# An mLSTM and ternary feed-forward block: masks, the split of x(1) and a value unit re-placed in the opening of the kernel

## The chip, the cores and the metric

One core of one Trainium2 chip runs one program. The metric is the device time of one execution in microseconds (us), as the median of several executions. Engines: TensorE (PE, with PEld for its weight loads), VectorE (DVE), ScalarE (ACT), GpSimd (POOL), and SyncE (SP), which here only issues DMAs.

## What is computed

For 16 sequences of 512 tokens with 512 features, in float32:

```
x = x + mlstm_layer(layernorm(x))        # 8 heads, q and k 256 wide, v 512 wide
x = x + ffn(layernorm(x))                # 512 -> 2048 -> 512, exact gelu, ternary weights

mlstm: i = cap(x Wig + big), f = cap(x Wfg + bfg), cap(z) = 15 tanh(z / 15)
       C_t = F C_{t-1} + I k v^T,  n_t = F n_{t-1} + I k,  h = (q C) / max(|q n|, exp(-m))
       y = (sigmoid(x Wog) * gamma * (h - mean) / sqrt(var + eps)) Wout      # mean, var per head
ternary: w -> sign(w) where |w| >= 0.7 mean|w|, else 0
```

## The kernel before

Each engine has a program written out by hand; they meet by semaphores alone, and each queue is strictly in order. A sequence is handled as 4 tiles (T = 4) of 128 tokens, the mLSTM in chunks of 128 tokens: within a chunk a head's scores (a 128x128 block for each chunk) are weighted with decays and masked to earlier tokens. float32 products are made of float16 halves (HI and LO) in three passes. The mLSTM part of sequence b runs beside the feed-forward part of sequence b - 1. Sequence 0 has no such partner: its mLSTM part runs beside the preparation of the weights, and this opening is what the change rewrites. `first` and `not run_f` mark it, and `isinstance(b, int) and b == 0`.

Preparation: w1 and w2 come as 16 pairs of row blocks. For pair q the division by the threshold (`small_gone`, VectorE, L1261, for w1; `small2_gone`, ScalarE, L826, for w2) is followed by `ternary_transpose(q)` on TensorE (into one of two banks of `pf`) and `ternary_out(q)` on ScalarE (L835), which writes the signs and frees the bank. The output weights go through `weights_out` (TensorE), `weights_hi` (ScalarE, L783) and `weights_lo` (VectorE, L1235).

The order around the change, for sequence 0:

- **Decays.** ScalarE exponentiates two heads at a time (`decay`, L1010). VectorE multiplies each head's scores from PSUM by its decays (`weigh`, L1475). GpSimd then masks two heads at a time (`earlier_only`, L653, an affine select over 128x1024), waiting until both have been weighed. `chunk_heads(0)` on TensorE waits for the last mask.
- **x(1).** VectorE normalises sequence 1 (`norm_apply`, L1297) and splits it (`split_x1`, L1307) into halves in `g32` and `qT`, ahead of the first `weigh`; SP moves them, transposed, to `xT` (`transpose_x1`, L544).
- **Head statistics.** `head_stats(0, j)` on VectorE (L1485), for chunks j = 0 to 3: sums of the columns (`hsum`), the norm (`den`) with a floor added as a tensor-scalar operation (L1526, and L1551 in `stats_in_bank` for j of 2 and 3), the centred heads (`cent`, L1528, L1547), `gated(j - 1)` (L1573) and the variance. Beside it for each j: ScalarE squares the centred heads (`squares`, L1051), GpSimd raises the variance to a power and multiplies (`head_norm`, L684 and L687), VectorE gates the product (L1579), ScalarE makes its high half (`gated_hi`, L1070), GpSimd its low half (`gated_lo`, L691), and SP transposes it to `hoT`, from which TensorE computes `project(0, j)`. `head_stats(0, j)` for j of 2 and 3 first waits for `gated_lo(j - 2)`.
- **TensorE** (`first_heads`, L2212): scores, transposes of w1 and w2 between the chunks, six filler products ahead of pair 5 and eighteen ahead of pair 10 (`busy_until`, L2194: products of an identity whose result is not used), the four projections, and before the third of these the gates and two value units of sequence 1 (`gates(1)`, `late_values(1, 1)`, `tokens(1, U_V, ...)`). The bank of `project(0, 3)` is freed by ScalarE's `value(1, 0)` (L953, L963), which is queued behind the exponential of sequence 1's gates (L873); that one needs `gate_minus(1)` on VectorE (L1342), which waits until the last transposed tile `hoT[3]` is there.

`busy_until` in the code:

```
def busy_until(q, times):
    pe.wait_ge(pf_free[q % 2], q // 2)
    keep_busy(pf[:, q % 2, :], times)
    ternary_transpose(q)
```

## Time and profile before

| what | value |
|---|---|
| median of 3 runs | 1740.2 us (1740.05 to 1741.62) |
| the profiled execution: its own time | 1742.3 us |
| its span | 1740.6 us |
| mean granted TensorE clock | 0.996 |
| TensorE busy | 1707.5 us, 98% of the span |
| VectorE, ScalarE, GpSimd busy | 1437.6, 1059.6, 606.6 us |
| end of the opening (start of `project(0, 3)`) | 116.01 us |

Times in the rows are microseconds from the span's start. "Granted clock" is TensorE's clock as the throttle let it through, 1 being 2.4 GHz and 0.5 being 1.2 GHz. A row of the timeline groups neighbouring instructions of one line; the bracket at its end is the time for which the engine was idle before it and what ended that.

### The profile page before, as it was taken

What the parts mean: (1) busy time and instruction counts of PE and PEld (TensorE: products, weight loads), DVE (VectorE), ACT (ScalarE), POOL (GpSimd) and SP (SyncE); (2) the same over time, 40 slices, a digit from 0 to 9 for tenths busy, and PEclk for the clock granted to TensorE, in tenths of its full rate; (3) what the DMA queues carried; (4) which work ended last, traced back from release to release, by engine and by line L of the source; (5) the groups of instructions that cost most, each with busy time, mean ns of one, the idle gap of its engine ahead of it and who ended that gap; (6) DMA issues with size and microseconds to landing.
All of it is one profiled execution on the core that took longest, in us unless ns stands there. A gap on an engine that the chain in (4) does not pass through costs nothing.

```text
span 1740.6 us, 31380 instructions
## 1 busy us (share of the span) xinstructions
PE 1707.5 (98%) x12028; PEld 841.4 (48%) x12028; DVE 1437.6 (83%) x2528; ACT 1059.6 (61%) x1769; POOL 606.6 (35%) x477
## 2 busy tenths in 40 slices
PE   6899999999999999999999999999999999999999
PEld 4554445444444444445444444444444444454455
DVE  7888788897888978789887888988789788886872
ACT  6978375473746638375573746648375573847643
POOL 1242514335241442514235241442514235241430
PEclk9999999999999999999999999999999999999999
DMA  8736253442725326253442725336262442625120
GB/s 321 219 89 167 58 141 72 117 120 56 170 60 127 87 80 160 58 154 59 120 117 56 171 60 126 87 92 152 55 161 61 110 119 56 148 59 132 33 55 25
DMA packets 294981, 187.45 MB, mean 108 GB/s; under 512 B 239136, under 2 KB 260640, under 8 KB 289712
## 3 DMA queue, kind: packets, MB, share of 16 engines
q1 hardware_dynamic: 293248, 182.30, 41.7%
q10 hardware_dynamic: 1584, 3.15, 0.5%
q8 instruction: 95, 1.56, 0.4%
q14 instruction: 54, 0.44, 0.1%
HBM read 96.47 MB, written 20.23 MB: 67 GB/s over the span
## 4 chain that ended last, share of the span: by engine, by line
PE 81%; DVE 8%; DMA 3%; SPq 3%; issue 2%; POOL 1%; ACT 1%; POOLq 0%; DVEq 0%; ACTq 0%
PE pf L2073 24%; PE pf L2057 22%; PE pa L1926 17%; PE pa L1902 7%; PE psh L1926 5%; SPq L530 2%; PE psh L2013 2%; DMA kT<-shared 1%; PE psh L1968 1%; PE psh L2047 1%; DVE gT L1633 1%; PE pa L2013 1%; DVE dec L1482 1%; PE pa L1893 1%; PE psh L2009 1%
## 5 line engine op out<-in xcount | busy, mean ns | idle before, releaser
L2073 PE MATMUL pf<-w2T,gT 128*128 128x512 f16 x2048 | 505.8, 379 | 0.0
L2057 PE MATMUL pf<-x2T,w1T 128*128 128x512 f16 x1920 | 422.0, 379 | 0.0
L2057 PEld LDWEIGHTS pf<-x2T,w1T 128*128 128x128 f16 x1920 | 185.4, 98 | 222.5
L2073 PEld LDWEIGHTS pf<-w2T,gT 128*128 128x128 f16 x2048 | 195.5, 97 | 177.0
L1633 DVE SCALAR_TENSOR_TENSOR gT<-g,wscale,gT 128x512 f16<-128x512 f32 x240 | 208.5, 871 | 22.5 <-ACT gT L1046 20.2
L1926 PE MATMUL pa<-wT,xT 128*128 128x512 f16 x960 | 212.8, 379 | 0.6 <-ACT sig L970 0.6
L1043 ACT ACTIVATE g<-pf,b1c 128x512 f32<-128x512 f32 x240 | 164.1, 684 | 72.5 <-PE pf L2057 56.6
L1046 ACT ACTIVATE gT<-g,wscale 128x512 f16<-128x512 f32 x240 | 173.3, 722 | 7.9
L1926 PE MATMUL pa<-wT,shared 128*128 128x512 f16 x768 | 176.2, 379 | 1.6 <-DMA shared<-qT 0.8
L1051 ACT ACTIVATE ktok<-kT 128x512 f32<-128x512 f32 x64 | 40.4, 631 | 216.4 <-DVE kT L1528 214.9
L1902 PE MATMUL pa<-xT,wT 128*128 128x512 f16 x768 | 171.4, 379 | 0.0
L1010 ACT ACTIVATE dec<-dec,gtok 128x128 f32<-128x128 f32 x512 | 154.4, 392 | 0.0
L1926 PEld LDWEIGHTS pa<-wT,xT 128*128 128x128 f16 x960 | 93.9, 98 | 113.6 <-ACT sig L970 1.1
L679 POOL TENSOR_TENSOR dec<-dec 128x1024 f16<-128x1024 f32 x30 | 71.9, 2398 | 200.4 <-ACT dec L1061 200.4
L1926 PE MATMUL psh<-wT,xT 128*128 128x512 f16 x576 | 129.7, 379 | 0.0
L702 POOL TENSOR_TENSOR x1b<-xres,b2r 128x512 f32<-128x512 f32 x64 | 80.6, 1269 | 125.2 <-DVE xres L1590 113.8
L684 POOL TENSOR_TENSOR hinv<-hvar,half 128x8 f32<-128x8 f32 x64 | 104.8, 1638 | 49.0 <-DVE hvar L1570 49.0
L691 POOL TENSOR_TENSOR qT<-kT,qT 128x512 f16<-128x512 f32 x64 | 74.1, 1157 | 132.5 <-ACT qT L1070 132.5
L1926 PEld LDWEIGHTS pa<-wT,shared 128*128 128x128 f16 x768 | 74.8, 98 | 92.4 <-DMA shared<-qT 1.8
L661 POOL TENSOR_SCALAR_AFFINE_SELECT dec<-dec 128x1024 f32<-128x1024 f32 x64 | 92.2, 1441 | 70.0 <-DVE dec L1482 69.8
L1902 PEld LDWEIGHTS pa<-xT,wT 128*128 128x128 f16 x768 | 74.5, 98 | 86.3
L651 POOL TENSOR_TENSOR rstd<-ve,half 128x4 f32<-128x4 f32 x16 | 16.6, 1037 | 279.6 <-DVE ve L1292 279.6
(246 smaller groups left out, 2705.2 us busy)
## 6 DMA issues: line engine op xcount, KB each, us to landing
dec<-gate_r SPq DMA_DIRECT2D x32, 1024.0 KB, 6.1
xin<-L_attn_x SPq DMA_DIRECT2D x16, 1024.0 KB, 6.0
out<-x1b SPq DMA_DIRECT2D x64, 256.0 KB, 2.3
xres<-L_attn_x SPq DMA_DIRECT2D x16, 512.0 KB, 4.3
xres<-L_attn_x SPq DMA_DIRECT2D x32, 256.0 KB, 3.0
qw<-gate_w SPq DMA_DIRECT2D x128, 48.0 KB, 2.0
s<-state_w SPq DMA_DIRECT2D x60, 97.5 KB, 2.4
qw<-kT SPq DMA_DIRECT2D x120, 48.0 KB, 2.0
```

The costliest lines, as they stand in the source:

```text
L661: nc.gpsimd.affine_select(out=rows_of, in_=rows_of, compare_op=ALU.is_ge, fill=0.0, base=0, pattern=[[0, 2 * T], [1, P]], channel_multipli ...
L684: nc.gpsimd.tensor_tensor(hinv[:, :], hvar[:, :], half[:, :], ALU.pow).then_inc(pool_a, 1)
L691: nc.gpsimd.tensor_tensor(head_parts[j % 2][:, LO, :], cent[j % 2], head_parts[j % 2][:, HI, :], ALU.subtract).then_inc(ho_lo[j], 1)
L702: nc.gpsimd.tensor_tensor(x1b[:, t, :], xres[:, t, :], b2r[:, :], ALU.add).then_inc(x1b_ok, 1)
L1010: last = nc.scalar.activation(dec[:, h, tok(j)], dec[:, h, tok(j)], ACT.Exp, bias=gtok[:, j, ROW_C, h:h + 1])
L1043: nc.scalar.activation(g32[:, f % 2, :], pf[:, use % 2, :], ACT.Gelu, bias=b1c[:, f:f + 1], scale=1.0 / X_SCALE).then_inc(pf_free[use % 2], 1)
L1046: nc.scalar.activation(gT[:, HI, f, :], g32[:, f % 2, :], ACT.Copy, scale=wscale[:, W_GELU:W_GELU + 1]).then_inc(g_hi, 1)
L1633: nc.vector.scalar_tensor_tensor(gT[:, LO, f, :], g32[:, f % 2, :], wscale[:, W_GELU:W_GELU + 1], gT[:, HI, f, :], ALU.mult, ALU.subtract) ...
L1902: last = nc.tensor.matmul(bank, wT[:, ws, k, col:col + P], xT[:, xs, :, k, :], start=(k == 0 and n == 0), stop=(k == KD - 1 and n == 2))
L1926: last = nc.tensor.matmul(bank, src[:, xs, k, :], wT[:, ws, k, col:col + D], start=(k == 0 and n == 0), stop=(k == KD - 1 and n == 2))
L2057: last = nc.tensor.matmul(bank, w1T[:, k, tok(f)], x2T[:, part, :, k, :], start=(k == 0 and part == HI), stop=(k == KD - 1 and part == LO))
L2073: last = nc.tensor.matmul(bank, gT[:, part, f, tok(t)], w2T[:, f, :], start=(f == 0 and part == HI), stop=(f == NF - 1 and part == LO), sk ...
```

## The change

In the opening alone, apart from one operation of the head statistics that changes its form in all sequences:

1. GpSimd masks the decays of sequence 0 as soon as ScalarE has made them, not the weighted scores; `weigh` waits for the mask, and `chunk_heads(0)` for the weighing.
2. The halves of x(1) lie in `xres`. The high half is made right after `norm_apply(1)`, the low half behind the fourth `weigh`. The loads of the residual into `xres` wait until x(1) has been transposed.
3. Head statistics: for j of 0 and 1 the centring takes the sum with a factor in one operation and stands ahead of the norm's steps; the floor is added as a tensor-tensor operation with the scalar broadcast; `weights_lo` of the first two output weights moves into `head_stats(0, 1)`, ahead of its centring.
4. TensorE: the second group of scores stands before the transposes of pairs 2 and 3. The unit `late_values(1, 1)` moves from ahead of `tokens(1, U_V, ...)` into the place of the eighteen fillers and writes to `pf`; ScalarE copies it there.
5. ScalarE: `decay(0, 6)` before `ternary_out(0)`; `squares(0)` before `small2_gone(9)`; `ternary_out(9)` up, `small2_gone(12)` and `(13)` down; the wait of `gated_hi(0, 0)` for x(1) goes.

```diff
-x1_halves = [... for part in (g32, qT)]
+x1_halves = [... for part in (xres[:, 0:T // 2, :], xres[:, T // 2:T, :])]
...
 def residual(b, tiles):                       # SP, sequence 0
                     sp.wait_ge(pa_fill, pa_filled(b, score_use(NH - 1)))
+                    sp.wait_ge(x1T_loaded, 32)
...
 def earlier_only(b, n):                       # GpSimd
-                for h in (2 * n, 2 * n + 1):
-                    if in_ps(h):
-                        pool.wait_ge(ps_free[h % 2], ps_done(b, h))
-                    else:
-                        pool.wait_ge(pa_free[h % 2], pa_done(b, score_use(h)))
+                if isinstance(b, int) and b == 0:
+                    pool.wait_ge(d_ok, 2 * n + 2)
+                else:
+                    for h in (2 * n, 2 * n + 1):
...
 def gates(b, fb):                             # ScalarE
-                value(b, 1)
+                if not (isinstance(b, int) and b == 1):
+                    value(b, 1)
...
 def opening():                                # ScalarE
                 decay(0, 4)
+                decay(0, 6)
                 ternary_out(0)
-                decay(0, 6)
...
 def gated_hi(b, j):                           # ScalarE
-                if isinstance(b, int) and b == 0 and j == 0:
-                    act.wait_ge(x1T_loaded, 32)
...
 def sequence(b, fb, ahead):                   # ScalarE
                     ternary_out(5)
+                    squares(b, 0)
                     small2_gone(9)
                     ternary_out(6)
                     small2_gone(10)
-                    squares(b, 0)
                     ternary_out(7)
                     weights_hi(*USES_OUT[0:2])
                     small2_gone(11)
...
                 if not run_f:
                     ternary_out(8)
-                    small2_gone(12)
+                    ternary_out(9)
                 squares(b, 2)
...
                 gated_hi(b, 1)
                 if not run_f:
-                    ternary_out(9)
-                    small2_gone(13)
+                    value(1, 1)
                     ternary_out(10)
+                    small2_gone(12)
                 squares(b, 3)
                 if not run_f:
                     ternary_out(11)
+                    small2_gone(13)
                 gated_hi(b, 2)
...
-            def split_x1():                   # VectorE
+            def split_x1_hi():
                 dve.wait_ge(xn_ok, 2 * T)
+                dve.wait_ge(s_abs, ABS_RES)
                 nc.vector.tensor_scalar(x1_halves[HI], xin[:, :, :], X_SCALE, None, ALU.mult).then_inc(x1_hi, 1)
+            def split_x1_lo():
                 dve.wait_ge(x1_hi, 1)
-                dve.wait_ge(qw_ok, 1)
...
 def weigh(b, n):                              # VectorE
-                dve.wait_ge(d_ok, at(b, NH, n + 1))
+                if isinstance(b, int) and b == 0:
+                    dve.wait_ge(masked, n // 2 + 1)
...
 def head_stats(b, j, ch, waiting=None, between=None):      # VectorE, sequence 0, j of 0 and 1
                     nc.vector.tensor_reduce(*columns)
                     nc.vector.scalar_tensor_tensor(den_of, *own_norm).then_inc(dve_a, 1)
+                    if between is not None:
+                        between()
+                    dve.wait_ge(dve_a, ch.next())
+                    nc.vector.scalar_tensor_tensor(by_head(cent[j % 2]), per_head(hsum[:, :], DHV), -1.0 / DHV, heads,
+                                                   ALU.mult, ALU.add).then_inc(cent_ok, 1)
+                    nc.vector.scalar_tensor_tensor(den_of, norms, -1.0, den_of, ALU.mult, ALU.max).then_inc(dve_a, 1)
+                    dve.wait_ge(dve_a, ch.next())
+                    norm_floor(ch)
+                    head_variance(b, j, ch, waiting)
+                    return
...
-                nc.vector.tensor_scalar(den[:, :], den[:, :], head_scale[:, 1:2], None, ALU.add).then_inc(dve_a, 1)
+                nc.vector.tensor_tensor(den[:, :], den[:, :], head_scale[:, 1:2].to_broadcast([P, NH]), ALU.add).then_inc(dve_a, 1)
...
 def sequence(b, fb, ahead):                   # VectorE
                     norm_apply(b + 1, range(T))
+                    split_x1_hi()
                     chunk_decay(b)
                     thresholds()
                     small_gone(0, 1)
                     key_tokens(b)
                     small_gone(2, 3)
-                    split_x1()
...
                     if not run_f and n == H4:
+                        split_x1_lo()
                         small_gone(4)
                     weigh(b, n)
...
                     head_stats(b, 0, ca, lambda: small_gone(7))
-                    head_stats(b, 1, ca)
-                    weights_lo(*USES_OUT[0:2])
+                    head_stats(b, 1, ca, None, lambda: weights_lo(*USES_OUT[0:2]))
                     head_stats(b, 2, ca)
...
 def chunk_state(b, j):                        # TensorE, j of 0
-                    pe.wait_ge(masked, at(b, NH // 2, NH // 2))
+                    if isinstance(b, int) and b == 0:
+                        for n in (H4, H4 + 1):
+                            pe.wait_ge(ps_free[n % 2], ps_done(b, n))
...
 def first_heads():                            # TensorE
                 scores(0, 0)
+                scores(0, 1)
                 ternary_transpose(2)
                 ternary_transpose(3)
-                scores(0, 1)
                 ternary_transpose(4)
...
                 weights_out(2, 3)
-                busy_until(10, 18)
+                x_ready(1)
+                pe.wait_ge(ps_free[1], at(1, PS_USES[1], 0))
+                pe.wait_ge(pf_free[1], 5)
+                token_products(pf[:, 1, :], xT[:, :, 1, :, :], C_V).then_inc(ps_fill, 1)
+                ternary_transpose(10)
+                pe.wait_ge(ps_free[1], at(1, PS_USES[1], 1))
                 ternary_transpose(11)
                 weights_ready(*USES_OUT)
                 project(0, 0)
                 ternary_transpose(12)
                 project(0, 1)
                 ternary_transpose(13)
-                x_ready(1)
                 gates(1)
                 ternary_transpose(14)
                 ternary_transpose(15)
-                late_values(1, 1)
                 tokens(1, U_V, xT[:, :, 0, :, :], C_V)
                 project(0, 2)
                 project(0, 3)
```

## Rows read from the trace of the kernel before

**Rows 1.** Stretches: length, busy us of PE, PEld, DVE, ACT, POOL, granted clock, DMA.
```profile
68.00:80.00 12.00, 7.12 (x86) 4.76 (x86) 10.83 (x18) 11.69 (x19) 5.06 (x4) 0.72 1.04 235
...
99.20:116.00 16.80, 15.90 (x104) 7.80 (x105) 11.24 (x23) 13.57 (x18) 9.45 (x8) 1.00 0.32 64
116.00:1736.00 1620.00, 1616.02 (x11291) 785.11 (x11292) 1345.48 (x2332) 966.62 (x1624) 574.88 (x438) 1.00 0.41 99
```

**Rows 2.** Timeline of TensorE: start, us, engine and line, operation, count, idle before.
```profile
76.73 2.77 PE L1850 MATMUL pf<-wT,ident 128*128 128x512 f16 x6
...
80.24 1.97 PE L2005 MATMUL pa<-vaug,dec 128*128 128x65 f32 x16 [0.17 <-POOL dec L661]
...
93.73 4.05 PE L1850 MATMUL pf<-wT,ident 128*128 128x512 f16 x18
...
116.01 2.75 PE L1926 MATMUL pa<-wT,shared 128*128 128x512 f16 x12 [0.60 <-ACT vaug L963]
```

**Rows 3.** Timeline of VectorE up to the last weighing.
```profile
59.74 0.17 DVE L1427 COPY fcol<-qw 128x6 f32<-128x6 f32 x1 [1.67 <-DMA qw<-gate_w]
...
62.52 1.42 DVE L1267 TENSOR_SCALAR x2T<-gT,w 128x1024 f16<-128x1024 f32 x2
...
67.11 1.22 DVE L1310 TENSOR_SCALAR g<-xin 128x2048 f16<-128x2048 f32 x1
68.37 2.29 DVE L1313 SCALAR_TENSOR_TENSOR qT<-xin,g 128x2048 f16<-128x2048 f32 x1
70.58 0.68 DVE L1482 SCALAR_TENSOR_TENSOR dec<-psh,dec 128x512 f32<-128x512 f32 x1
...
73.08 1.28 DVE L1482 SCALAR_TENSOR_TENSOR dec<-pa,dec 128x512 f32<-128x512 f32 x2
...
77.20 1.28 DVE L1482 SCALAR_TENSOR_TENSOR dec<-pa,dec 128x512 f32<-128x512 f32 x2
```

**Rows 4.** The masks of sequence 0, all instructions of line 661 up to 120 us.
```profile
L661 POOL TENSOR_SCALAR_AFFINE_SELECT dec<-dec x4: 1093/1292/1482, 73.3 to 78.6; 128x1024 f32<-128x1024 f32 x4
```

**Rows 5.** VectorE: the divisions by line, then its timeline in chunks 1 and 3.
```profile
L1267 DVE TENSOR_SCALAR x2T<-gT,w x8: 742/748/1578, 62.5 to 85.1; 128x1024 f16<-128x1024 f32 x8
...
88.51 0.96 DVE L1526 TENSOR_SCALAR den<-den,head_scale 128x8 f32<-128x8 f32 x1
...
90.37 0.69 DVE L1579 SCALAR_TENSOR_TENSOR kT<-kT,sig 128x512 f32<-128x512 f32 x1
...
91.78 1.41 DVE L1248 SCALAR_TENSOR_TENSOR wT<-pa,gcol,wT 128x512 f16<-128x512 f32 x2
...
107.06 0.69 DVE L1579 SCALAR_TENSOR_TENSOR kT<-kT,sig 128x512 f32<-128x512 f32 x1 [0.50 <-POOL kT L687]
```

**Rows 6.** Timeline of VectorE and GpSimd in sequence 1, side by side in time.
```profile
188.72 2.10 DVE L1530 SCALAR_TENSOR_TENSOR den<-den,head_scale 128x8 f32<-128x8 f32 x1
...
188.13 2.66 POOL L679 TENSOR_TENSOR dec<-dec 128x1024 f16<-128x1024 f32 x1 [0.42 <-ACT dec L1061]
```

**Rows 7.** Timeline of ScalarE.
```profile
60.39 2.44 ACT L1010 ACTIVATE dec<-dec,gtok 128x128 f32<-128x128 f32 x8
...
79.05 1.14 ACT L833 ACTIVATE x2T<-gT,w 128x1024 f16<-128x1024 f32 x1
80.11 1.02 ACT L844 ACTIVATE w1T<-pf 128x1024 f16<-128x1024 f16 x1
...
87.49 1.26 ACT L795 ACTIVATE wT<-pa,gcol 128x512 f16<-128x512 f32 x2
...
102.36 0.63 ACT L1070 ACTIVATE qT<-kT 128x512 f16<-128x512 f32 x1 [0.32 <-DVE kT L1579]
```

**Rows 8.** GpSimd by groups, 56 to 120 us: count, busy us, mean ns, idle before.
```profile
L684 POOL TENSOR_TENSOR hinv<-hvar,half 128x8 f32<-128x8 f32 x4 | 6.6, 1638 | 6.6 <-DVE hvar L1570 6.6
...
L691 POOL TENSOR_TENSOR qT<-kT,qT 128x512 f16<-128x512 f32 x4 | 4.6, 1159 | 7.4 <-ACT qT L1070 7.4
L687 POOL TENSOR_TENSOR kT<-kT,hinv 128x512 f32<-128x512 f32 x4 | 4.2, 1042 | 0.3
```

More of the change, by code:

```diff
@@ L195, in block_program @@
         square = head_sum[:, :, 0:DHV]
-        x1_halves = [part[:, :, :].bitcast(F16).rearrange("p g s -> p (g s)").rearrange("p (t d) -> p t d", d=D) for part in (g32, qT)]
+        x1_halves = [part[:, :, :].bitcast(F16).rearrange("p g s -> p (g s)").rearrange("p (t d) -> p t d", d=D) for part in (xres[:, 0:T // 2, :], xres[:, T // 2:T, :])]
         q16 = (kT[:, :, :].bitcast(F16).rearrange("p g s -> p (g s)")[:, 0:2 * HG * LATE]
@@ L403, in block_program @@
         wbank = [ps[:, 0, :], pf[:, 0, :], pf[:, 1, :], ps[:, 1, :], pa[:, 0, :], pa[:, 1, :]]
+        ABS_RES = 3
         USES_V, USE_GATE, USES_QK, USES_O, USES_OUT = range(4), 4, range(5, 9), range(9, 13), range(13, 17)
@@ L958, in value @@
                     act.wait_ge(ps_fill, at(b, PS_FILLS, F_V + 1))
-                    bank, free = ps[:, 1, :], ps_free[1]
+                    bank, free = pf[:, 1, :] if isinstance(b, int) and b == 1 else ps[:, 1, :], ps_free[1]
                 else:
@@ L1480, in weigh, with head_stats @@
                     dve.wait_ge(pa_fill, pa_filled(b, score_use(n)))
-                dve.wait_ge(d_ok, at(b, NH, n + 1))
+                if isinstance(b, int) and b == 0:
+                    dve.wait_ge(masked, n // 2 + 1)
+                else:
+                    dve.wait_ge(d_ok, at(b, NH, n + 1))
                 nc.vector.scalar_tensor_tensor(dec[:, n, :], score_bank(n), SCORE_SPLIT, dec[:, n, :],
                                                ALU.mult, ALU.mult).then_inc((ps_free if in_ps(n) else pa_free)[n % 2], 1)
-            def head_stats(b, j, ch, waiting=None):
+            def head_stats(b, j, ch, waiting=None, between=None):
                 if not (isinstance(b, int) and b == 0 and j == 0):
@@ L1532, in head_stats, with norm_floor @@
                 head_variance(b, j, ch, waiting)
+            def norm_floor(ch):
+                nc.vector.tensor_tensor(den[:, :], den[:, :], head_scale[:, 1:2].to_broadcast([P, NH]), ALU.add).then_inc(dve_a, 1)
+                dve.wait_ge(dve_a, ch.next())
+                nc.vector.scalar_tensor_tensor(den[:, :], den[:, :], head_scale[:, 2:3], den[:, :], ALU.mult, ALU.mult).then_inc(dve_a, 1)
+                dve.wait_ge(dve_a, ch.next())
             def in_bank(b, j):
@@ L1977, in chunk_state @@
                         take_pa(b, U_H0 + g)
-                    pe.wait_ge(masked, at(b, NH // 2, NH // 2))
-                    if not (isinstance(b, int) and b == 0):
+                    if isinstance(b, int) and b == 0:
+                        for n in (H4, H4 + 1):
+                            pe.wait_ge(ps_free[n % 2], ps_done(b, n))
+                    else:
+                        pe.wait_ge(masked, at(b, NH // 2, NH // 2))
                         pe.wait_ge(vlo_ok, at(b - 1, T, T))
```

6 lines of the change are left out of this document (5 added, 1 removed).

## Prediction

> **What bounds the kernel now.** The table of stretches comes first [rows 1]. From 116 us to the end TensorE is busy 1616.02 of 1620 us at full clock, so nothing behind 116 us can be shortened by this change: it can only move the moment at which that block begins. Before it TensorE is not the bound: 7.12 of 12 us are busy from 68 to 80 us, at a granted clock of 0.72.
>
> TensorE's own rows tell what holds it there [rows 2]. The heads of the first chunk begin at 80.24, released by the last mask on the decays. Eighteen fillers run from 93.73 for 4.05 us and compute nothing. `project(0, 3)` begins at 116.01 after 0.60 us of waiting for ScalarE's copy of the values of sequence 1 out of a bank. That copy stands behind the exponential of sequence 1's gates, which needs the last transposed head tile, which comes from `gated(0, 3)` on VectorE at 107.06 [rows 5]. Between 107.06 and 116.01 lie 8.95 us of dependent steps that the change leaves alone (ScalarE's and GpSimd's halves, a transposing DMA, gate steps, exponential, copy). So what decides is when `gated(0, 3)` runs; the four chunks before it are a chain through VectorE, ScalarE and GpSimd. The two moved pieces of TensorE work count only if that chain keeps up.
>
> **Up to the first heads.** Removed ahead of the first weighing: both halves of the split of x(1), 67.11 to 70.58 on VectorE, 3.4 us [rows 3]. The high half (1.22 us) goes into 1.67 us in which VectorE waits for a DMA before 59.74: free. If that cover were gone it would cost its 1.22. The low half (2.29) goes behind the fourth weighing. Its old place has no cover, its new one lies beside the scores of heads 4 to 7, for which VectorE would wait about 1 us anyway.
>
> The masks now need only the decays. ScalarE makes the first pair by 62.83 [rows 7], the second, after a copy of 0.5 and as many exponentials, by about 65.8, where VectorE runs the threshold divisions and, between them, the two key operations [rows 3]. Masks and divisions block one another: a division takes 742 ns undisturbed and 1578 at worst, the worst one standing beside a mask [rows 5], and a mask 1093 to 1482 [rows 4]. The price of a mask that gets in ahead of such an instruction is therefore 0.84 us (1578 less 742); the other bound is 0 (VectorE first, GpSimd waits, which hurts nobody: a mask has some microseconds to spare). Two masks fall there. I take both at 0.85, so 1.7 us, since both orders of arrival put the mask between two queued VectorE instructions. First weighing: 70.58 - 3.4 + 1.7 = 68.9. Fourth ends 3.8 later (as now, 70.58 to 74.36) at 72.7; low half to 75.0; division 4 to 75.7; weighings 4 to 7 take 2.5, to 78.2, against 78.4 now [rows 3].
>
> TensorE meanwhile: scores of heads 4 to 7 begin with the end of the fourth weighing, and now scores and the transposes of one pair of w1 fill the time from there to the fillers, 74.36 to 76.73, 2.3 us with their releases [rows 2, 3]. Pairs 2 and 3, transposed ahead of the scores before, now stand behind them, so pair 2 is done at 72.7 + 2.3 = 75.0, and ScalarE can write the signs of pairs 2 and 3 only then, at 1.0 us apiece [rows 7]: 76.0 and 77.0. The six fillers wait for the second of these. From the first filler to the first head it is 3.5 us now, of which 0.17 is the wait for the mask, with the clock at its lower level (six fillers in 2.77 against eighteen in 4.05) [rows 2]: 77.0 + 3.3 = 80.3. The first heads begin at 80.2 or 80.3, as now: **the wait for the masks is gone, and the signs ahead of the fillers take its place.** Bounds: 79.1 if no mask gets in the way and the clock is up, 81 if the lower clock lasts into the heads.
>
> **Chunk 0.** Centring comes two steps sooner (0.65 us), which only makes ScalarE's squares ready sooner; VectorE's own queue is one 0.2 us instruction shorter. Gain 0.2.
>
> **Chunk 1, the costly place.** `weights_lo` of the first two output weights (1.41 us) [rows 5] moves from behind chunk 1 into its middle, ahead of the centring. It waits for ScalarE's `weights_hi`, at 87.49 now [rows 7]. ScalarE's list up to there has changed too: the squares of chunk 0 stand before `small2_gone(9)`, and ScalarE, a strict queue, sits idle for them from about 82.8 to 84.0. From there: squares 0.6 (as long as a high half, 0.63), then `small2_gone` 1.04, signs 0.92 and both once more (spacings of instructions of 1.14 and 1.02) [rows 7], so `weights_hi` begins at about 88.5 and the first is done at 89.2. VectorE reaches the wait at 87.5 and idles 1.7; the two `weights_lo` end at 90.7, the centring runs from 90.6 (now 89.50, right behind the 0.96 us instruction) and `gated(0, 0)` at 91.9 against 90.37 now [rows 5]. Behind the waiting VectorE instruction stand the centring, the squares and variance of chunk 1 and `gated(0, 0)`. The shorter list gives 0.9 of it back (0.96 to 0.17, and one of 0.16). The net is **+1.5**.
>
> **Chunks 2 and 3.** One turn of the loop is: `gated` 0.69, ScalarE's high half 0.63, GpSimd's low half 1.16, power 1.64, product 1.04 [rows 5, 7, 8], with some 0.2 of releases: 5.4 us. Today the turns take 5.63 (90.37 to 107.06 in three). So once the loop binds a turn can shrink by 0.2 and no more: -0.4 for two. The other way, ScalarE's list now has `ternary_out(11)` and `small2_gone(13)` together before `gated_hi(2)`, and also the copy of the moved unit: `gated_hi(2)` starts about 0.9 late (bounds 0 and 1.6). The new wait on TensorE, for ScalarE's copy of the moved unit, has `ternary_transpose(11)` and `project(0, 0)` behind it; the copy is queued behind `gated_hi(0, 1)`, so it is there near 99.3, while `project(0, 0)` waits for `weights_lo` on VectorE until about 100.3 in any case: nothing.
>
> **Queues passed.** On SP the transposition of the low half now waits for 75.0 instead of 70.5, and the load of x(2), the third and fourth loads of w2 rows and the residual wait behind it, the residual also for its landing, about 80. The first reader of x(1) is the moved unit near 95, of the w2 rows a ScalarE instruction near 100, of the residual the first output near 104. On GpSimd the masks pass nothing. I cost all this at 0; without that cover each would cost the 4.5 us of its lateness at most.
>
> The other saving announced, the floor of the norm as a tensor-tensor operation, is worth little. The 0.96 us instruction at 88.51 stands beside GpSimd's product (0.23 is its normal length) [rows 5], but VectorE instructions with two SBUF operands are stretched by GpSimd just as well: the 128x8 one at 188.72 takes 2.10 and ends with GpSimd's 188.13 + 2.66 [rows 6]. The new form has two SBUF operands, so in chunks 2 and 3 I count nothing for it. The Trainium skill (SBUF — State Buffer, "SBUF: two separate sides") says the same in general: the pair of ports shared with GpSimd is an exclusive lock, also for a VectorE operation with two SBUF inputs against a GpSimd one that reads SBUF. By the row alone, which shows tensor-scalar operations stretched and says nothing of the new form, chunks 2 and 3 would gain up to 0.5 each until the loop binds, about 0.6 together, and the sum would be +1.7 where I take +2.3.
>
> **Sum.** 0 (start) - 0.2 + 1.5 - 0.4 + 0.9 = +1.8; the same schedule laid out instruction by instruction with these durations, which also carries the small idle gaps, gives +2.6. I take +2.3. TensorE: 3.9 us of fillers go, the unit of 2.6 us leaves the stretch before `project(0, 2)`; both turn into waiting, for signs 9 before the unit and for the gates' bank and the values' copy before 116. All behind `project(0, 3)` moves with it, in one piece.
>
> The profiled execution took 1742.3 us around its span of 1740.6, 2.1 above the median of the runs, 1740.2. It would become 1744.6; the median 1742.5. About 0.2%, 3.5 us, is what a measurement of this kernel tells from no change.
>
> **Rivals.**
> *No contention.* Masks slip into gaps, `weights_hi` is early enough for VectorE to idle 0.5 instead of 1.7: the start wins 1.1, chunk 1 loses 0.3. Sum about 0 to -0.5, plus 0.9 on ScalarE: 1740.5. For it: masks now mostly delay themselves. Against: the 1.09 us masks have no gap in VectorE's row from 62.5 to 66.
>
> *The chain shortens as meant.* Start -1.1, chunk 0 -0.2, chunk 1 -0.9 (`weights_lo` finds its input ready), two turns -0.2 each, ScalarE in time: -2.6, 1737.6. TensorE would allow it: it has 2.6 + 0.6 to give. Against: ScalarE is busy 11.69 of 12 us up to 80 us [rows 1], and the stretch behind has got one more operation for it.
>
> *The clock falls.* With fillers gone and the unit moved, TensorE idles over 2 us before the unit and over 4 in all between 106 and 118. From 68 to 80 us, after TensorE had waited twice for signs, the mean granted clock is 0.72 [rows 1]; at levels of 1 and 0.5 (2.4 and 1.2 GHz) that is 0.56 of 12 us, 6.7 us, at the lower one. If it drops again as `project(0, 3)` starts and stays down as long, half of 6.7 us, 3.4, is lost in the saturated block: 2.3 + 3.4, 1745.9. It decides from the point at which the drop reaches past 118; a drop that ends earlier falls into waiting and costs little. Against it: before 118 TensorE still has two projections and the values to do, where before 73 it had next to nothing.
>
> **Chances.** Forecast 0.55, no contention 0.18, shorter chain 0.10, clock 0.17. Shorter chain lies mostly inside 3.5 us, so faster by over 0.2% gets 0.04; slower gets the clock's 0.17 and 0.03 of the forecast's tail. Range: 1738.5 leaves out most of the shorter chain, 1746.0 takes in the clock's value.
>
> **What would show it.** Right: first mask about 63, a VectorE instruction beside it stretched by 0.8; first heads near 80.2; a VectorE wait for ScalarE `wT` near 87.5 to 89.3; `gated(0, 0)` near 92, and `project(0, 3)` at 118 to 118.6 after some 2 us idle; same work behind it. Wrong: heads at 79 or a `project(0, 3)` at or before 116, or a granted clock under 1 behind it.

## The result, and the profile after

The changed kernel takes 1742.1 us (median of 20 runs, 1741.35 to 1745.21), the kernel before 1740.0 us (20 runs alongside, 1739.18 to 1741.62). The medians are 2.1 us apart; the ratio, 1.0015 with a 95% interval of 1.0009 to 1.0022, is nearer to the means, which are 2.7 us apart, since the changed kernel has some high times. That is inside the 3.5 us that were set as "no change", but the interval leaves 1 out, so the changed kernel is slower by a little. The forecast was 1742.5.

One warning for reading the two profiles: the profiled execution of before was 2.1 us above its median, that of after is the fastest of its twenty (1741.35, span 1739.6). Span against span, the changed kernel looks 1.0 us shorter. The opening, which the change rearranges, is the part to compare, counted from a moment that both kernels have: the copy of the gate columns, `fcol`, at 59.74 before and at 59.19 now. Below, "from fcol" means counted from there. Before, the copy starts when a DMA has landed, and now right behind the high half of x(1); counted from the normalising of sequence 1 just ahead of it, it comes 3.57 and 3.09 us later, in a second profile of each kernel 3.11 and 3.27. So this origin hides some tenths at most.

The table of stretches of the kernel after (length, busy us of PE, PEld, DVE, ACT, POOL, granted clock, DMA), to be put beside [rows 1]:

```profile
68.00:80.00 12.00, 7.23 (x100) 5.81 (x101) 10.92 (x19) 10.04 (x17) 2.18 (x2) 0.86 1.00 205
80.00:99.20 19.20, 14.99 (x177) 12.77 (x177) 15.41 (x36) 16.72 (x22) 8.30 (x7) 1.00 0.60 202
99.20:116.00 16.80, 13.47 (x92) 6.45 (x91) 10.63 (x21) 13.38 (x17) 9.37 (x8) 1.00 0.42 64
116.00:1736.00 1620.00, 1616.67 (x11296) 785.53 (x11296) 1342.37 (x2333) 966.94 (x1625) 571.08 (x438) 1.00 0.40 99
```

Behind 116 us the rows show TensorE with the same work (1616.67 us busy, 1616.02 before). Between 99.2 and 116 us TensorE has 2.4 us less to do than before, and the stretch has not become shorter for it. TensorE's own timeline says why:

```profile
75.84 0.61 PE L1872 MATMUL pf<-ident,x2T 128*128 128x128 f16 x8 [0.35 <-ACT w1T L849]
76.67 1.47 PE L1878 MATMUL pf<-wT,ident 128*128 128x512 f16 x6 [0.22 <-ACT w1T L849]
...
78.48 1.95 PE L2036 MATMUL pa<-vaug,dec 128*128 128x65 f32 x16
...
93.64 2.75 PE L1954 MATMUL pf<-wT,xT 128*128 128x512 f16 x12 [2.10 <-ACT w2T L849]
...
111.86 2.75 PE L1954 MATMUL pa<-wT,shared 128*128 128x512 f16 x12 [1.08 <-DVE qT L1348]
116.66 2.75 PE L1954 MATMUL pa<-wT,shared 128*128 128x512 f16 x12 [2.05 <-ACT vaug L969]
```

The first heads no longer wait for a mask and start 19.29 us from fcol (20.50 before). The moved unit has taken the fillers' place at 93.64, behind an idle gap of 2.10 us that waits for signs. `project(0, 3)` stands 57.47 us from fcol (56.27 before), now behind 2.05 us of waiting for ScalarE's copy, where it was 0.60 [rows 2]. So the start won 1.2 us, and 2.4 us were lost between the first heads and `project(0, 3)`. VectorE's timeline shows where:

```profile
61.96 1.42 DVE L1272 TENSOR_SCALAR x2T<-gT,w 128x1024 f16<-128x1024 f32 x2
63.29 1.85 DVE L1424 TENSOR_TENSOR ktok<-kT 128x768 f32<-128x768 f16 x1
...
66.13 2.24 DVE L1272 TENSOR_SCALAR x2T<-gT,w 128x1024 f16<-128x1024 f32 x2
68.29 0.68 DVE L1493 SCALAR_TENSOR_TENSOR dec<-psh,dec 128x512 f32<-128x512 f32 x1
...
76.03 1.28 DVE L1493 SCALAR_TENSOR_TENSOR dec<-pa,dec 128x512 f32<-128x512 f32 x2
...
87.73 1.41 DVE L1253 SCALAR_TENSOR_TENSOR wT<-pa,gcol,wT 128x512 f16<-128x512 f32 x2 [1.14 <-ACT wT L800]
89.06 0.68 DVE L1533 SCALAR_TENSOR_TENSOR kT<-hsum,ktok 128x512 f32<-128x512 f32 x1
...
90.32 0.69 DVE L1607 SCALAR_TENSOR_TENSOR kT<-kT,sig 128x512 f32<-128x512 f32 x1
...
94.85 0.79 DVE L1579 TENSOR_TENSOR den<-den,head_scale 128x8 f32<-128x8 f32 x1
...
101.56 0.69 DVE L1607 SCALAR_TENSOR_TENSOR kT<-kT,sig 128x512 f32<-128x512 f32 x1
...
107.59 0.69 DVE L1607 SCALAR_TENSOR_TENSOR kT<-kT,sig 128x512 f32<-128x512 f32 x1
```

Two instructions at the front are stretched, one for each of the first two masks (62.83 and 65.74 on GpSimd). At 87.73 `weights_lo` holds VectorE 1.14 us for ScalarE, and the centring of chunk 1 (89.06) stands behind it. From the first heads to `gated(0, 0)` it is now 11.84 us against 10.13 [rows 2, 5]. A turn is the time from one `gated` to the next. The last, 101.56 to 107.59, takes 6.03 us, where it took 5.42 before (101.64 to 107.06); the reason is on ScalarE:

```profile
101.87 1.14 ACT L838 ACTIVATE x2T<-gT,w 128x1024 f16<-128x1024 f32 x1
102.91 0.62 ACT L1074 ACTIVATE qT<-kT 128x512 f16<-128x512 f32 x1
```

The upper row is `small2_gone(13)`. `gated(0, 2)` ended at 102.25, and its high half could begin only at 102.91; before it began 0.03 us after its input [rows 5, 7]. GpSimd's power for chunk 3 is queued behind the low half of chunk 2, so `gated(0, 3)` inherits the delay. VectorE gets to it no sooner: the residual and the statistics of `project(0, 1)`, which is itself late, stand ahead and end at 107.52, GpSimd's product at 107.48.

### The profile page after: what moved, and what is told of

It reads as the page before. It is cut to its first block, busy times and chain, and to the rows that moved or that the text cites. A ratio compares the mean times of both kernels' runs of the same rounds, so it can differ in the third digit from the quotient of the medians.

```text
span 1739.6 us, 31338 instructions
## 1 busy us (share of the span) xinstructions
PE 1703.2 (98%) x12010; PEld 839.4 (48%) x12010; DVE 1433.4 (82%) x2526; ACT 1059.2 (61%) x1769; POOL 602.7 (35%) x477
## 4 chain that ended last, share of the span: by engine, by line
PE 88%; DVE 3%; ACT 1%; issue 1%; POOL 1%; DMA 1%; SPq 1%; POOLq 0%; DVEq 0%; ACTq 0%
PE pf L2104 24%; PE pf L2088 23%; PE pa L1954 19%; PE pa L1930 8%; PE psh L1954 6%; PE psh L2044 2%; PE psh L1996 1%; PE psh L2078 1%; PE psh L1977 1%; PE pa L2044 1%; PE pa L1921 1%; PE psh L2040 1%; SPq L532 1%; POOL qT L696 0%; DMA kT<-shared 0%
## 5 line engine op out<-in xcount | busy, mean ns | idle before, releaser
L666 POOL TENSOR_SCALAR_AFFINE_SELECT dec<-dec 128x1024 f32<-128x1024 f32 x64 | 90.9, 1421 | 66.5 <-DVE dec L1493 61.5
```

The source lines that it names most:

```text
L666: nc.gpsimd.affine_select(out=rows_of, in_=rows_of, compare_op=ALU.is_ge, fill=0.0, base=0, pattern=[[0, 2 * T], [1, P]], channel_multipli ...
```

## The experiments

Twelve kernels, in three groups. Each ran 11 times, beside the kernel before on the same chip, whose medians were 1740.65, 1740.44 and 1740.26 us. "Start" is first heads from fcol, "end" is `project(0, 3)` from fcol, in the kernel's profiled execution.

| kernel | median (range) | ratio to before, 95% | start | end |
|---|---|---|---|---|
| base_again | 1740.58 (1740.04 to 1741.26) | 0.9999 [0.999, 1.0008] | 20.49 | 56.16 |
| after_again | 1743.58 (1741.56 to 1744.86) | 1.0014 [1.0005, 1.0023] | 19.87 | 57.94 |
| fill_idle | 1743.04 (1740.95 to 1746.04) | 1.0017 [1.0008, 1.0025] | 20.00 | 58.12 |
| wlo_back | 1743.91 (1741.92 to 1746.01) | 1.0017 [1.0008, 1.0026] | 19.41 | 57.82 |
| fill_early | 1741.79 (1740.30 to 1744.61) | 1.0012 [1.0003, 1.0021] | 19.24 | 57.39 |
| order | 1740.04 (1738.57 to 1743.18) | 1.0003 [0.9994, 1.0012] | 19.29 | 54.86 |
| masks_only | 1742.55 (1741.51 to 1743.57) | 1.0013 [1.0004, 1.0021] | 22.43 | 58.19 |
| order_early | 1739.66 (1738.74 to 1742.83) | 0.9998 [0.9989, 1.0007] | 19.27 | 54.51 |
| fill_both | 1742.27 (1741.66 to 1743.38) | 1.0011 [1.0003, 1.002] | 19.31 | 58.84 |
| order_fill | 1739.62 (1737.63 to 1742.03) | 0.9999 [0.999, 1.0008] | 19.30 | 54.77 |
| before_order | 1740.91 (1739.75 to 1747.26) | 1.0007 [0.9998, 1.0016] | 20.53 | 56.45 |
| s13_later | 1743.93 (1741.04 to 1747.26) | 1.0019 [1.0011, 1.0028] | 19.29 | 56.99 |

**base_again and after_again**, no edit: how far one profile can be trusted.

> The kernel before, once more, for a second trace. Both theories: 1740, ratio 1.000. What it tells apart is where two executions of one program differ. If the differences lie in the opening, project(0, 3) starts 0.5 us or more away from 116.0; if they lie in single pauses of TensorE behind it, project(0, 3) starts at 115.5 to 116.5 and the rest of the difference is in pauses.

> The changed kernel, once more. Its 20 times fall in two groups, 13 at 1741.4 to 1742.3 and 7 at 1743.1 to 1745.2. Theory clock: the upper group are executions in which TensorE's clock drops in the idle time before project(0, 3) and stays down into the saturated block (1.7 or 3.4 us lost); again about a third of the times lie 1.5 to 3.4 us above the rest. Theory chain only: the groups were chance, all times within 1 us. Median 1742 either way. In the trace project(0, 3) starts at 116.6 if the clock is up again by 76 us, near 118 if it stays down to 79.

The kernel before gives 56.16 where its first profile gave 56.27: its chain repeats to 0.1 us. The changed kernel doesn't repeat as well, 57.94 against 57.47. One row of TensorE's timeline in after_again shows what varies:

```profile
93.95 4.44 PE L1954 MATMUL pf<-wT,xT 128*128 128x512 f16 x12 [2.62 <-ACT w2T L849]
```

And the stretch around it in the same execution, in the columns of the table of stretches:

```profile
90.00:100.00 10.00, 7.14 (x48) 3.86 (x46) 8.42 (x22) 7.09 (x11) 6.11 (x5) 0.83 0.29 53
```

The unit that takes 2.75 us elsewhere took 4.44, at a mean granted clock of 0.83: after 2.62 us of idling the clock was at its lower level (1.2 GHz) for part of it. It cost little here, because TensorE has slack up to `project(0, 3)`.

**masks_only**: the kernel before with only the three pieces of the change that release the masks early; x(1) is split where it was.

```diff
-for h in (2 * n, 2 * n + 1):
+if isinstance(b, int) and b == 0:
+    pool.wait_ge(d_ok, 2 * n + 2)
...
-dve.wait_ge(d_ok, at(b, NH, n + 1))
+if isinstance(b, int) and b == 0:
+    dve.wait_ge(masked, n // 2 + 1)
...
-pe.wait_ge(masked, at(b, NH // 2, NH // 2))
+if isinstance(b, int) and b == 0:
+    for n in (H4, H4 + 1):
+        pe.wait_ge(ps_free[n % 2], ps_done(b, n))
```

> The kernel before with the masks on the decays alone (GpSimd waits for the decays, weigh for the mask, chunk_heads(0) for the weighings); the split of x(1) and all orders stay. Contention theory: two masks fall beside the divisions and key operations and stretch VectorE by 0.85 each, the first weighing begins at 72.3 instead of 70.6, the last ends at 80, and the first heads begin at 80.2 to 80.6, no earlier than now: 1740.3 to 1741. If the masks slip into gaps: the first heads begin 0.5 to 0.9 earlier, at 79.3 to 79.7 (the transposes of pair 5 are then last), 1739.5 to 1740.

The start came 1.9 us *later* than before (22.43 against 20.49) and the kernel 2.1 us slower by its median, beyond the 1741 at which the expectation ended. VectorE's timeline in masks_only:

```profile
63.22 1.85 DVE L1419 TENSOR_TENSOR ktok<-kT 128x768 f32<-128x768 f16 x1
...
66.05 2.24 DVE L1270 TENSOR_SCALAR x2T<-gT,w 128x1024 f16<-128x1024 f32 x2
68.22 1.21 DVE L1313 TENSOR_SCALAR g<-xin 128x2048 f16<-128x2048 f32 x1
69.46 3.06 DVE L1316 SCALAR_TENSOR_TENSOR qT<-xin,g 128x2048 f16<-128x2048 f32 x1
72.44 0.68 DVE L1488 SCALAR_TENSOR_TENSOR dec<-psh,dec 128x512 f32<-128x512 f32 x1
```

Here a third mask costs as well: the low half of the split takes 3.06 us for 2.29 [rows 3]. Together the three lengthen VectorE's way to the first weighing by 0.90, 0.83 and 0.77 us, which is the whole 2.50 us by which it is later (13.34 from fcol, 10.84 before). So early masks alone make the start later. In the change the first weighing is at 9.10, and the 4.24 us between the two kernels are the two rows of the split, which stand elsewhere there. The rival of no contention is refuted by these rows.

**wlo_back**: `weights_lo` again behind chunk 1.

```diff
-head_stats(b, 1, ca, None, lambda: weights_lo(*USES_OUT[0:2]))
+head_stats(b, 1, ca)
+weights_lo(*USES_OUT[0:2])
```

> The changed kernel with weights_lo of the first two output weights back behind head_stats(0, 1), nothing else. If its wait in the middle of chunk 1 is what costs (my +1.5), gated(0, 0) comes near 88.5 instead of 90.3, and project(0, 3) 0.5 to 1.5 us earlier: 1740.6 to 1741.6. If ScalarE's order of work is the next limit, gated(0, 0) is early but gated_hi(0, 2) is not, and the gain at the end is 0.5 or less (1741.6).

The step itself was named rightly: `gated(0, 0)` is back at 10.16 us from the first heads (10.13 before, 11.84 in the change). But the end was at 57.82, no better than with the change. VectorE's timeline shows the gain given back in the next turn:

```profile
87.32 1.58 DVE L1533 SCALAR_TENSOR_TENSOR kT<-hsum,ktok 128x512 f32<-128x512 f32 x1
...
89.47 0.69 DVE L1607 SCALAR_TENSOR_TENSOR kT<-kT,sig 128x512 f32<-128x512 f32 x1
90.71 0.69 DVE L1592 TENSOR_REDUCE hsum<-ktok 128x8 f32<-128x512 f32 x1 [0.54 <-ACT ktok L1057]
91.43 1.02 DVE L1598 SCALAR_TENSOR_TENSOR hvar<-hsum,den 128x8 f32<-128x8 f32 x1
92.37 1.40 DVE L1253 SCALAR_TENSOR_TENSOR wT<-pa,gcol,wT 128x512 f16<-128x512 f32 x2
...
96.60 0.69 DVE L1607 SCALAR_TENSOR_TENSOR kT<-kT,sig 128x512 f32<-128x512 f32 x1
```

The turn takes 7.13 us (89.47 to 96.60) where the change has 5.62. Two rows account for most of it. First, VectorE waits 0.54 us for the squares of chunk 1, which stand in ScalarE's list behind two high halves and `small2_gone(11)`. By that wait the 128x8 operation at 91.43 falls beside GpSimd's low half (91.27 to 92.42) and takes 1.02 us, where it takes 0.17 in the change, a moment ahead of the low half. (`hsum` at 94.53, 0.78 us for 0.17, adds nothing: it stands beside the product in the place of the floor, which costs as much in the change.) So the wait was moved, not removed, and it brought a second loss with it. That ScalarE's order is behind both is what the run order tests. The profiled execution of wlo_back, 1745.63 us, also caught what the clock rival said. First a row of TensorE's timeline:

```profile
117.72 4.29 PE L1955 MATMUL pa<-wT,shared 128*128 128x512 f16 x12 [2.06 <-ACT vaug L969]
```

Then the stretch from 118 to 124 us of that execution:

```profile
118.00:124.00 6.00, 6.00 (x22) 2.35 (x21) 4.11 (x7) 1.50 (x2) 2.32 (x2) 0.72 0.01 3
```

After 2.06 us of waiting the clock stood at its lower level (1.2 GHz) at the start of the block where TensorE is saturated. In these 6 us the mean granted clock is 0.72; at levels of 1 and 0.5 that is 3.4 us at the lower one, and half of it, 1.7 us, is lost for good (an estimate from this row). The spans agree: from the start of `project(0, 3)` to the end of the span it is 1626.2 us here and 1622.6 to 1624.6 in the other thirteen profiles.

**s13_later**: the change with `small2_gone(13)` behind `gated_hi(0, 2)`.

```diff
-                    small2_gone(13)
                 gated_hi(b, 2)
+                    small2_gone(13)
```

> The changed kernel with small2_gone(13) on ScalarE behind gated_hi(0, 2) instead of ahead of it, nothing else. My term of +0.9: gated_hi(0, 2) begins at once behind gated(0, 2), near 102.3 instead of 102.9, and project(0, 3) 0.6 to 0.7 us earlier: median 0.6 lower than the changed kernel, the upper group of times as large as before. If it only moves the work ahead of gated_hi(0, 3): no gain.

`gated_hi(0, 2)` now starts at 102.41, with its input, and the end is 0.5 us earlier than in the change (56.99 against 57.47). Of this, 0.27 is the last turn (5.76 for 6.03); 0.21 lies behind `gated(0, 3)`, where a wait for a DMA is shorter (2.33 for 2.54), which no row ties to the edit. The turn does not come back to 5.42 because the product is there at 107.0 now and VectorE gets to `gated(0, 3)` only at 107.4, behind the statistics of `project(0, 1)`. The median did not follow: 1743.93, with five of eleven runs at 1742.42 or below and six at 1743.93 or above. The term is there in the trace, smaller at the end of the opening than its 0.66 us at `gated_hi(0, 2)`, and smaller than what else moves the median.

**order**: wlo_back, and ScalarE's list of the opening put in the order in which the results are wanted (several calls to a line here).

```diff
-sigmoids(b)
 small2_gone(8); ternary_out(5)
+sigmoids(b)
 squares(b, 0)
-small2_gone(9); ternary_out(6); small2_gone(10); ternary_out(7)
-weights_hi(*USES_OUT[0:2]); small2_gone(11); squares(b, 1)
+small2_gone(9); small2_gone(10); ternary_out(6); small2_gone(11)
+weights_hi(USES_OUT[0]); squares(b, 1)
 gated_hi(b, 0)
-ternary_out(8); ternary_out(9); squares(b, 2)
-weights_hi(*USES_OUT[2:4])
+weights_hi(USES_OUT[1]); ternary_out(7); ternary_out(8); ternary_out(9)
+weights_hi(USES_OUT[2]); squares(b, 2); weights_hi(USES_OUT[3])
 gated_hi(b, 1)
-value(1, 1); ternary_out(10); small2_gone(12)
-squares(b, 3); ternary_out(11); small2_gone(13)
+small2_gone(12); value(1, 1); ternary_out(10); small2_gone(13)
+squares(b, 3); ternary_out(11)
 gated_hi(b, 2)
```

> The changed kernel with weights_lo of the first two output weights back behind head_stats(0, 1) and ScalarE's list of the opening in another order: what the chain of heads waits for (weights_hi(0), squares, gated_hi) ahead of divisions and signs that nobody waits for yet. If ScalarE's order is the limit that the run wlo_back met, gated_hi(0, 0) begins 1 us earlier than 91.0, gated_hi(0, 2) near 100.5 to 101.5 instead of 102.9, and project(0, 3) 2 to 3 us earlier, at 114 to 115: median 1740 to 1741. If the loop through VectorE, ScalarE and GpSimd is the floor (5.4 us a turn) the gain stays under 1 us.

The end is at 54.86 us from fcol, 2.6 earlier than the change and 1.4 earlier than before. From the first heads to `gated(0, 0)` it is 9.94 us, and the three turns take 16.67 (17.27 in the change). The stretch from 80.00 to 99.20 us of order, in the columns of the table of stretches:

```profile
80.00:99.20 19.20, 16.61 (x184) 13.24 (x182) 18.29 (x41) 18.60 (x24) 10.65 (x8) 1.00 0.64 205
```

ScalarE is busy 18.60 of 19.20 us where the change has 16.72, and VectorE 18.29 where it has 15.41: more of the chain's work fits in. The median, 1740.04, is 2.1 us below that of the changed kernel's twenty runs, which were taken at another time, and 0.4 below that of before beside it: no difference that can be told from none. The pair wlo_back and order differs in ScalarE's list alone, and its ends are 3.0 us apart: with `weights_lo` behind chunk 1, that list is what makes the opening late. The new list with `weights_lo` left in the middle of chunk 1 was not run, so how the change's own 1.7 us in chunk 1 divide between the list and the place of `weights_lo` is not shown.

**before_order**: the kernel before with the same list (its unit `value(1, 1)` stays in `gates(1)`).

> The kernel before with ScalarE's new order alone; masks, split, statistics, scores and fillers as before. If the order would have helped without the change: gated(0, 0) at 89.5 to 90 instead of 90.4 and project(0, 3) 0.5 to 1.5 us earlier, 1739 to 1740. If VectorE's own queue is what limits the kernel before (turns of 5.63 us without idle time) it moves by less than 0.3 us: 1740.4.

No gain: end 56.45 against 56.16 and 56.27, median 1740.91. In the kernel before, ScalarE's order costs nothing. The first two turns take 5.63 or 5.64 us in before, in this run and in order. What holds them there, VectorE's own list or the loop through ScalarE and GpSimd, this run does not tell: in the profile of before VectorE has no idle time from `gated(0, 0)` to `gated(0, 2)`, and `gated_hi(0, 1)` starts only 0.04 us behind its input. The list matters only together with the rest of the change.

**fill_idle**: the change with fillers in TensorE's four gaps (4, 3, 4 and 8 products whose result is not used).

```diff
 weights_out(2, 3)
+pe.wait_ge(pf_free[0], 5)
+keep_busy(pf[:, 0, :], 4)
...
 ternary_transpose(12)
+pe.wait_ge(ph_free, at(1, PH_USES, 0))
+keep_busy(ps[:, 0, :], 3)
...
+keep_busy(ps[:, 0, :], 4)
 project(0, 2)
+keep_busy(ps[:, 0, :], 8)
 project(0, 3)
```

> The changed kernel with 19 fillers put in TensorE's new idle times (4 before the moved unit, 3 before project(0, 1), 4 before project(0, 2), 8 before project(0, 3), 0.216 us each, each stretch shorter than the idle time measured there). Theory clock: the upper group of times goes, median 0.3 to 1 us lower than the changed kernel, near 1741.5. Theory chain only: nothing moves, within 0.3 us. If the fillers get in the way: up to 0.9 us slower.

No gain: 1743.04, where the clock theory had 1741.5, and the same spread. The fillers of the last gap filled it almost to the end (the idle time before `project(0, 3)` fell from 2.05 to 0.25 us). They did not delay it: the end is at 58.12 because the first heads are at 20.00, with a mean granted clock of 0.71 from 76 to 80 us, and from the heads on it takes as long as in the change. **fill_early** instead puts 12 fillers into the gap behind the scores of the first four heads.

```diff
 scores(0, 0)
+pe.wait_ge(ps_free[0], ps_done(0, 0))
+keep_busy(ps[:, 0, :], 12)
 scores(0, 1)
```

> The changed kernel with 12 fillers between the two groups of scores (from the first weighing, about 69 us, to 71.6), where TensorE idles 4.2 us. Theory clock: the lower clock between 67.5 and 77.8 is what lengthens the opening and, in the upper group of times, reaches into the heads; with the fillers the first heads begin at 78.0 to 78.5 in place of 78.5 to 79.8, and the median falls by 1 to 1.5 us, from 1743 to about 1741.7. Theory chain only (weighings and signs, not the clock, set the first heads): unchanged, within 0.3 us, or slower by as much as the fillers delay the scores (0.2).

The lower clock of 72 to 76 us is gone from the trace (a mean of 1.00 for 0.57), and the start is the same, 19.24 us: the transposes of w1 behind the scores now wait 0.92 us for a division on VectorE. Six runs lie at 1740.30 to 1741.79 and five at 1742.75 and above, so the spread is still there. The median, 1741.79, is the one that the clock theory expected, but its reason is missing: neither the start nor the end (57.39) has moved. **fill_both** is both edits together.

> The changed kernel with both sets of fillers, the 12 between the scores and the 19 in the later idle times. Apart, the late ones left the median as it was and the early ones lowered it by about 1.5 us while 5 of 11 times stayed 2 to 3 us above the rest. Theory clock: each set leaves the other place open; with both the upper group goes, at most 1 of 11 times above 1743 and a median of 1740.8 to 1741.6. If the spread has another cause, 3 to 5 of 11 times are above 1743 again.

All eleven runs lie between 1741.66 and 1743.38, the narrowest of the changed kernels, but not lower: 1742.27, where the clock theory had at most 1741.6, and two times above 1743, where it had one. The end is at 58.84, and a row of VectorE's timeline in fill_both says why:

```profile
115.14 0.42 DVE L1355 TENSOR_SCALAR qT<-qT 8x512 f32<-8x512 f32 x1 [3.88 <-DMA shared<-qT]
```

The change waits 2.54 us there. The transposing DMA was issued at 110.13 and its reader started 5.01 us later, in the other thirteen profiles 3.22 to 3.67 us later. Without that the end would be near 57.5, as in the change, so the fillers delay nothing. The profiled execution, 1743.22, is one of the two high ones: here a high time goes with a late DMA, at full clock from 56 us on.

**order_early** (order and fill_early) and **order_fill** (order_early, 4 fillers ahead of `project(0, 2)` and 6 ahead of `project(0, 3)`) look for a version that beats both kernels.

> The two edits together: ScalarE's new order with weights_lo back, and the 12 fillers between the groups of scores. If both theories hold their gains add, since one moves the start of the heads and the other shortens the way from there: project(0, 3) at 113 to 114.5, median 1739 to 1740.3, below the kernel before by 0.3 to 1.5 us. If only one holds it equals the better of the two.

> The run order_early with 10 more fillers in the last two idle times (4 before project(0, 2), 6 before project(0, 3), in a bank that nothing reads). Theory clock: its one slow time of 11 goes, the median stays at 1739.2 to 1739.8, about 0.8 us under the kernel before. Theory chain only: the same median, and now and then a time above 1742.

Their medians are 1739.66 and 1739.62, 0.8 and 0.6 us below before beside them, with ratios whose intervals hold 1. They are the best of the study, 2.5 us better than the change, and can't be told from the kernel before. The fillers add nothing that the traces show: the first heads are at 19.27 and 19.30, as in order (19.29), and the way to `gated(0, 3)` is the same. In order_early only one run of eleven is above 1741; `project(0, 3)` is 1.7 us earlier than in before, and the median shows half of that.

## Why the prediction was right, point by point

The direction was right, and so were the places at which time is won and lost. The sum was off, and that the median came out 0.4 us from the forecast is in part luck. The forecast took +2.3 at `project(0, 3)`; its terms add up to +1.8, and the layout that gave +2.6 is not shown. The two profiles have +1.2 and +1.7. The medians are 2.1 us apart, and in the later pair 2.9, so about 1 us of the measured difference is not in the opening as profiled. All times are counted so that the varying stretch before fcol drops out.

| term | forecast | after | after_again |
|---|---|---|---|
| first heads | 0 | -1.2 | -0.6 |
| heads to `gated(0, 0)` | +1.3 | +1.7 | +1.7 |
| three turns to `gated(0, 3)` | +0.5 | +0.6 | +0.7 |
| `gated(0, 3)` to `project(0, 3)` | 0 | +0.1 | -0.1 |
| sum | +1.8, taken +2.3 | +1.2 | +1.7 |

- **Masks, 0.85 each.** Right, in place and size. The first stretched a tensor-tensor operation from 0.95 to 1.85 us, the second a pair of divisions from 1.42 to 2.24: 0.90 and 0.82. First weighing 9.10 us from fcol, forecast 9.16; end of the last weighing 18.12, forecast 18.46.
- **"The signs ahead of the fillers take its place."** Right: the six fillers begin 17.48 us from fcol (76.67), forecast 17.26, released by ScalarE's signs.
- **First heads at 80.2: the step that failed.** What failed is its last term, "77.0 + 3.3", with the clock at its lower level. In the profile of after the eight transposes before the fillers take 0.61 us and the six fillers 1.47, where they took 2.77 [rows 2]: the clock was back up, and from the first filler to the head it is 1.81 us. Counted as before (fcol at 59.74) the heads are at 79.0. The lower bound, 79.1, was given for no mask in the way and the clock up; the masks were in the way, and the bound was passed all the same. In after_again the six take 2.11 us, between the two, and the heads are at 79.6. So the term is -1.2 and -0.6 where the sum has 0, and it should have been a range there.
- **Chunk 1, +1.5 (-0.2 for chunk 0).** Right in its place, low in size: 1.7 for both, where 1.3 was forecast. The wait at `weights_lo` was 1.14 us, forecast 1.7, since VectorE came to it 8.1 us behind the first heads and not 7.3; in the profile of before it is 7.95 us to the same step, so 87.5 was 0.7 too early. wlo_back shows the whole 1.7 coming back here, and lost again in the next turn.
- **Turns, -0.4.** Wrong: the first two take 5.62 as before. (The three turns of before, 90.37 to 107.06, average 5.56; the 5.63 holds for the first two, and the third takes 5.42.) The loop does bind, with VectorE waiting 1.19 us for GpSimd at 92.99, and its length is 5.62, not the 5.4 that was added up with 0.2 of releases. What the sum left out is the floor. It stands beside GpSimd's product (100.20 to 101.24), ends with it (100.51 to 101.27), and the 0.23 us operation behind it still has to run, so `gated` starts 0.32 us behind the product. In the third turn of before, where no floor stands there, it starts 0.11 us behind it.
- **`gated_hi(2)` +0.9.** Mechanism right, size 0.66; s13_later gives back 0.27 in the turn, since VectorE's list is the next limit.
- **The floor as tensor-tensor, nothing in chunks 2 and 3.** Right: 0.79 and 0.76 us beside GpSimd's product, 0.76 and 0.76 before, and 0.17 where GpSimd is idle. The Trainium skill (SBUF — State Buffer, "SBUF: two separate sides") puts it as an exclusive lock that holds also for a VectorE operation with two SBUF inputs against a GpSimd one that reads SBUF. The trace agrees: the floor at 94.85 ends at 95.64, the product beside it at 95.62.
- **Queues passed, 0.** No row of after shows a wait for the transfers that were moved back.
- **The clock rival.** It happens, but it is not shown to explain the change's high times. The times of after lie in two groups, thirteen at 1741.35 to 1742.34 and seven at 1743.15 to 1745.21, and those of before don't. One high execution of wlo_back has the lower clock for 3.4 us from about 118 us on and 1.7 us lost by it; the rival had put 3.4 lost. The mean granted clock of each run tests the rest: 1.7 us lost in the saturated block lower it by 0.001. In s13_later it is 0.9954 on the mean for the five low times and 0.9937 for the six high ones, and the run of before_order at 1747.26 has 0.992 where its fast ones have 0.995 and 0.996: there the clock is about as low as the times are high. In after both groups have 0.9946, and two of the upper one, 1743.64 and 1744.75, have 0.996 like the fastest; in after_again it is no lower for the high times either. What lifts those is open. fill_both shows one other cause, a late DMA.
- **No contention; the chain shortens as meant.** The first is refuted by masks_only. The second needs the list of order, whose opening ends 1.3 to 1.4 us ahead of before in the trace; the median, 0.4 below, can't be told from it.
- **What would show it.** In the time of before, the first mask is at 63.4, VectorE's wait from 87.1 to 88.3 and the idle time before `project(0, 3)` 2.05 us, with the clock at 1 behind it: as forecast. `gated(0, 0)` is at 90.9 (near 92 forecast) and `project(0, 3)` at 117.2, in after_again at 117.7 (118 to 118.6 forecast). Heads at 79 had been named as a sign of being wrong, and they came: up to the first heads the account failed in its last term, behind them it held.

What stays open: the upper group of the change's times, and with it about 1 us of the difference of the medians; why order_fill, with its gaps filled, still has three runs near 1742; why the clock falls in some executions and not in others with the same gaps; why the DMA of fill_both landed late.

## What to carry to other kernels

When work is taken off an engine that isn't the bound ahead of a saturated block, follow each strictly ordered queue in the chain and ask in which order its results are wanted: here one list of ScalarE decided 3.0 us (wlo_back against order), and undoing the visible wait on VectorE alone moved the loss into the next turn. A GpSimd operation that blocks VectorE is best placed where VectorE waits or works from PSUM: the third and fourth mask of the change run beside weighings from PSUM, in 1.09 us each, and the weighings keep their 0.68. The price of a bad place can be read from one stretched row. Compare two kernels by distances from a moment that both share, and by medians: the profiled executions of one kernel differ by as much as the change is worth.

## What the runs showed of the hardware that was not expected

- Two profiled executions of the same kernel before differ by 2.1 us (1742.3 and 1740.21): 0.9 of it lies before fcol (59.74 and 58.85) and about 1.1 behind `project(0, 3)`, whose chain in between differs by 0.1.
- The lower clock in the opening comes at different places in executions of one program: in the profile of after the stretch from 68 to 80 us has a mean granted clock of 0.86, in that of after_again 0.59, and there also one of 0.83 from 90 to 100 us. Gaps of about 2 us on TensorE came before each of the late ones; most of the profiled executions have the same gaps without it (fill_early idles 2.62 us before the same unit, which then takes its 2.75 us).
- One and the same transposing DMA has its reader started 3.22 to 3.67 us after its issue in thirteen profiles and 5.01 us in fill_both.
- A GpSimd mask stretches a VectorE instruction by 0.77 to 0.90 us (after and masks_only), about as much on a tensor-tensor operation as on divisions, while GpSimd's 128x8 power stretches none of those beside it. The same `hsum` operation takes 0.17 us beside the power in after and 0.78 beside the product in wlo_back. First the power in GpSimd's timeline of after:

```profile
92.86 1.64 POOL L689 TENSOR_TENSOR hinv<-hvar,half 128x8 f32<-128x8 f32 x1
```

And VectorE's timeline of after beside it, with operations of 0.21 and 0.17 us at their usual length:

```profile
93.60 0.21 DVE L1570 SCALAR_TENSOR_TENSOR den<-gtok,head_scale,psh 128x8 f32<-128x8 f32 x1
93.85 0.17 DVE L1573 TENSOR_SCALAR hsum<-hsum 128x8 f32<-128x8 f32 x1
```
